# Moving the weight tiles by 128 bytes within each SBUF partition, in a fused state-space and mixture-of-experts layer

## What is computed

```python
x = _layernorm(x + attn(x))      # state-space part: z, Win, scan over 8 heads, gate, Wout
x = _layernorm(x + ffn(x))       # mixture of 12 experts, top 3 per token
# attn: z = x@Wz; X,B,C,dt = x@Win; y = ssd_scan(...) + D*X; (y * (silu(z)@Wzg)) @ Wout
# ffn, dense over the experts:
h = gelu(sum_e (x @ W1[e].T) * dw1[:, e])     # W1[e]: 512 x 128
y = sum_e (h @ W2[e].T) * dw2[:, e]           # W2[e]: 128 x 512
y = y + dw3 @ b2
```

## The kernel before, in words

| tile | start, bytes | modulo 256 | modulo 512 |
|---|---|---|---|
| before_lines | 16512 | 128 | 128 |
| w1_hi, w1_lo | 16640, 41216 | 0 | 256 |
| w2_hi, w2_lo | 65792, 90368 | 0 | 256 |
| wbc_hi, wbc_lo | 114944, 115456 | 0 | 256 |
| wz_hi, wz_lo | 115968, 116992 | 0 | 256 |
| wx_hi, wx_lo | 118016, 120064 | 0 | 256 |
| wzg_hi, wzg_lo | 122112, 126208 | 0 | 256 |
| wout (first tile after the weights) | 130304 | 0 | 256 |
| xT_hi, xT_lo | 141568, 143616 | 0 | 256 |
| fbuf (x1 is its first 2048 bytes) | 199168 | 0 | 0 |
| sp_hi, sp_lo | 209920, 218112 | 0 | 0 |
| dwpad | 227200 | 128 | 384 |
| a_hi, a_lo | 228192, 228320 | 96, 224 | 352, 480 |

## Time and profile before

### The profile page before, as it was taken

How to read it: one execution, slowest core, us unless ns; L and a number is a source line. 1 busy time by engine, 2 the same in 40 slices (tenths; PEclk the granted TensorE clock), 3 DMA queues, 4 the chain that set the end, 5 groups by cost and what they waited for, 6 DMA issues and landing times.

```text
span 1540.9 us, 25335 instructions
## 1 busy us (share of the span) xinstructions
PE 1525.7 (99%) x8646; PEld 1250.4 (81%) x8646; DVE 1115.0 (72%) x3113; ACT 598.1 (39%) x1360; POOL 658.3 (43%) x751
## 2 busy tenths in 40 slices
PE   9999999999999999999999999999999999999998
PEld 7778888888888888888788888888888888887886
DVE  7677776877768687686776768777686776767755
ACT  6643424425244351533525244242443515335130
POOL 6671623616145270643616336162451705436040
PEclk9999999999999999999999999999999999999999
DMA  6340312314023140321403123040230403214020
GB/s 180 100 148 29 118 42 67 100 29 135 18 77 90 30 137 15 103 71 46 120 11 125 45 61 106 28 132 21 72 95 29 138 15 96 76 39 128 14 78 7
DMA packets 81456, 114.53 MB, mean 74 GB/s; under 512 B 10144, under 2 KB 37296, under 8 KB 81328
## 3 DMA queue, kind: packets, MB, share of 16 engines
q1 hardware_dynamic: 81328, 112.92, 24.6%
HBM read 107.76 MB, written 5.13 MB: 73 GB/s over the span
## 4 chain that ended last, share of the span: by engine, by line
PE 93%; POOL 3%; DVE 1%; issue 1%; DMA 1%; SPq 0%; ACT 0%; POOLq 0%; DVEq 0%
PE exp_bank L247 23%; PE exp_bank L249 22%; PE exp_bank L248 22%; PE mix_bank L896 4%; PE mix_bank L922 3%; PE mix_bank L247 3%; PE mix_bank L249 3%; PE mix_bank L904 3%; PE mix_bank L248 3%; PE mix_bank L793 1%; PE turn_bank L1249 1%; PE mix_bank L525 1%; PE mix_bank L739 1%; PE mix_bank L1013 1%; POOL Wt L856 1%
## 5 line engine op out<-in xcount | busy, mean ns | idle before, releaser
L1190 POOL TENSOR_TENSOR sp_lo<-fbuf,sp_hi 128x512 fp32r<-128x512 f32 (+2 forms) x201 | 243.4, 1214 | 176.9 <-ACT sp_hi L1186 106.9
L247 PE MATMUL exp_bank<-w_hi,sp_hi 128*128 128x512 f32 x768 | 304.0, 396 | 0.8 <-POOL sp_lo L1242 0.8
L247 PE MATMUL exp_bank<-sp_hi,w_hi 128*128 128x512 f32 x764 | 303.5, 397 | 0.1
L249 PE MATMUL exp_bank<-w_hi,sp_lo 128*128 128x512 f32 x768 | 299.7, 390 | 0.0
L248 PE MATMUL exp_bank<-w_lo,sp_hi 128*128 128x512 f32 x768 | 298.9, 389 | 0.0
L249 PE MATMUL exp_bank<-sp_hi,w_lo 128*128 128x512 f32 x764 | 298.3, 391 | 0.0
L248 PE MATMUL exp_bank<-sp_lo,w_hi 128*128 128x512 f32 x764 | 297.8, 390 | 0.0
L1289 DVE SCALAR_TENSOR_TENSOR acc<-exp_bank,dw,acc 128x128 f32<-128x128 f32 x384 | 132.4, 345 | 137.2 <-PE exp_bank L249 136.6
L1186 ACT CAST sp_hi<-fbuf 128x512 fp32r<-128x512 f32 (+2 forms) x203 | 120.0, 592 | 272.5 <-DVE fbuf L1156 216.5
L856 POOL TENSOR_TENSOR Wt<-Wt,Gh 128x512 f32<-128x512 f32 x128 | 184.8, 1445 | 21.0 <-DVE Wt L848 21.0
L247 PEld LDWEIGHTS exp_bank<-sp_hi,w_hi 128*128 128x128 f32 x764 | 143.7, 188 | 38.2 <-issue 8.9
(11 more groups left out here) (267 smaller groups left out, 2286.1 us busy)
## 6 DMA issues: line engine op xcount, KB each, us to landing
row_b<-dw_rows SPq DMA_DIRECT2D x189, 256.0 KB, 3.3
seg_b<-dA_rows SPq DMA_DIRECT2D x124, 256.0 KB, 3.5
ctd<-cum_rows SPq DMA_DIRECT2D x128, 96.0 KB, 3.2
x_in<-in_x SPq DMA_DIRECT2D x16, 256.0 KB, 2.8
result<-acc SPq DMA_DIRECT2D x15, 256.0 KB, 2.2
fbuf<-in_W1T SPq DMA_DIRECT2D x12, 256.0 KB, 3.5
acc<-in_W2T SPq DMA_DIRECT2D x5, 256.0 KB, 3.5
x_in<-in_W2T SPq DMA_DIRECT2D x5, 256.0 KB, 2.8
```

Of the source, the lines that this page charges most:

```text
L247: nc.tensor.matmul(ps, s_hi, m_hi, start=start and j == 0, stop=False, skip_group_check=onto)
L249: last = nc.tensor.matmul(ps, s_lo, m_hi, start=False, stop=stop and j == n - 1, skip_group_check=onto)
L1190: sig("xw_lo", on.tensor_tensor(lo[:, cols], wide[e % 2][:, cols], hi[:, cols].bitcast(F32), ALU.subtract))
```

## The change

The number and the order of the tiles are kept, except for one unused tile of 128 bytes per partition. It stood ahead of the weights and now stands behind them.

```diff
@@ -91,7 +91,6 @@
-        sb("before_lines", [P, 32])
         w1_hi, w1_lo = sb("w1_hi", [P, E, HID], F32R), sb("w1_lo", [P, E, HID], F32R)
         w2_hi, w2_lo = sb("w2_hi", [P, NH, E * D], F32R), sb("w2_lo", [P, NH, E * D], F32R)
@@ -100,6 +99,7 @@
         wx_hi, wx_lo = sb("wx_hi", [P, DI], F32R), sb("wx_lo", [P, DI], F32R)
         wzg_hi, wzg_lo = sb("wzg_hi", [P, NK, DI], F32R), sb("wzg_lo", [P, NK, DI], F32R)
 
+        sb("half_line", [P, 32])
         wout = sb("wout", [P, NQ, D])
```

## The result

The changed kernel takes 1567.5 us (median of 4, 1567.48 to 1568.39), against 1542.8 us for the kernel before on the same chip: 24.7 us more, a ratio of 1.016 (95% interval 1.0148 to 1.0172). I had predicted no change, with a range that ended at 1547.8.

A forecast was written before the change was run, and what follows sets the result against it. PE was taken as the bound, with 5,328 fp32r matmuls at 226.7 ns making 1,208 us, 78% of the span. All terms were 0, so the forecast stayed at the median, 1543.3 us, range 1540.6 to 1547.8.

The forecast's parts named there:

- Terms 3 and 4: Splitting W1 and W2 once: 0, or 1.3 us without cover; tiles behind the weights, which keep their bytes: 0.
- term 2: Weights as moving operand, 2,496 matmuls: no change in start distance, 0; bounds -33 us to +4.2 us.
- term 1: Weights as stationary operand, 2,832 loads: no delay from the new position, 0; a third block's 156 us was excluded.
- load covered by 39 ns: Stationary loads take 188 ns, one starts every 226.7 ns, so 39 ns are free before a load delays a matmul.
- Rival B: Moving W2 or wx starting mid-block touches nine blocks, not eight: 1.7 ns each, 4.2 us, 1547.5 us; chance 0.12.
- dearer form: Rival B with the stationary side paying too: 1.7 ns on 5,328 matmuls, 9.1 us, 1552.4 us; within Rival B's 0.12.
- Rival A: TensorE's reads of both operands collide at present; half a block apart frees up to 71 us, 1472 us; chance 0.07.
- the 13.4 ns: Part of the 226.7 ns between fp32r matmul starts above the 213.3 ns that 512 columns take at 2.4 GHz.

The follow-up runs named there:

- the first map: Separate kernel computing none of the layer: streams of 44 fp32r matmuls, only the slices' start bytes varied; 226.6 ns at 256 and 0, 232.7 with the stationary at 128.

## Why the prediction was wrong

**What held.** The bound, the count and the sensitivity did: PE is the bound with and without the change, 5,328 fp32r matmuls carry it, and the loss is 4.9 ns on the distance between their starts. Terms 3 and 4 were 0: the growth of the distances accounts for the whole loss, and nothing behind the weights moved.

**The step that failed is term 2, and with it term 1.** Both were put at 0; the pairs of the trace give 12.0 us where the weight moves (term 2) and 13.8 us where it is stationary (term 1). In term 2 I took 0 because "the rows show the distance blind to position where they can tell". They couldn't tell. The rows compared differences of 0 and 256 bytes, and the first map has 226.6 ns at 256 (L44), as at 0, against 232.7 at 128 (L41). All fp32r rows of 512 columns of before had the same difference modulo 256, so they were one sample and not two. From that I should have drawn that no row tested the change.

**The nearest rows were of another kind.** Term 1 leaned on L1123, whose 512-byte stationary operand starts at 128 under a moving one at 0. It is a single float32 transpose beside other short matmuls, so it neither streams nor is fp32r. In the result its matmuls are at 272 ns, and float32 streams had 429 ns at both positions. Nor was its 1 ns a measure: its loads have a median of 143 ns in the result in place of 138, with both of its operands where they were. The load of the large matmuls stays at 188 ns in the changed kernel too. What changes is when the next matmul starts. I read "load covered by 39 ns" as "position of the stationary operand free"; only-W1-at-128 costs 12 us and shows that it isn't. The 39 ns were no measure of the cover either, since loads of 188 to 192 ns start 112 to 120 ns apart in streams of 128 and 256 columns.

**Rival B had the right sign and the wrong mechanism.** It let only moving operands pay, 1.7 ns for a ninth block. Taking the pad out puts all streams mid-block at no cost. The price was 4.9 ns and both roles paid it: 5,328 x 4.9 = 26 us, not 4.2. Even its dearer form, 1552.4 us, was 15 us short. Its remark that leaving equal positions "can lose a privilege which no row tests" was the true state of the evidence, and should have carried more chance and a wider upper end.

**Rival A and the page.** Half a block between the operands doesn't take the 13.4 ns away, and with 512 columns none of the 63 other positions gets below 226.7. Two reads that get in each other's way are not excluded by this: which offset is costly did turn out to depend on how the two operands lie to each other. The Trainium skill's "TensorE: Matmul & The Clock Gate" (Step-by-step: what each phase is for) says that loading the next tile's weights doesn't steal read bandwidth from the running matmul. No run measures the bandwidth, but the two operands are not independent in effect: moving only the start of W1, the stationary one, costs 6.6 ns a matmul in the stretch shown and 5.1 over its 2,304 matmuls. Whether that is the ports or something behind them, no run tells. The page's gap of N/2.4 + 2.5 ns (Back-to-back issue gap), 215.8 ns for 512 columns, wasn't reached at any position.

What stays open is the mechanism inside. Most settled distances are multiples of 6.67 ns (226.7, 233.3 and 240.0 are 34, 35 and 36 of them; 113.3, 120.0 and 173.3 are 17, 18 and 26), or are repeating patterns whose sum is one, as 229 + 238 = 467 = 70 x 6.67. That looks like a handover between matmuls that waits for its turn, but only the arithmetic points to it.

## What to carry to other kernels

Where fp32r matmuls of 512 columns run back to back and TensorE is the bound, start the stationary and the moving tile at equal bytes modulo 256: common starts at 0, 64, 128 and 192 all settled at 226.7 ns, and one small tile allocated between them was enough to lose 1 to 2% here. Before calling rows evidence that a quantity doesn't matter, check that they really differ in it, in the period that may count. The distance between starts shows the loss at once; PE's share of the span (99%) and of the chain (93%) doesn't. And the length of a load isn't the time that has to be free for it.

## What the runs showed of the hardware that I had not expected

- The cost depends on the difference of the two starts modulo 256, with its sign: 228.9 ns with the moving operand 64 above, 233.3 with it 192 above. The load's own time (188 ns) and the granted clock (1.00) don't show it.
- It isn't a matter of how far: 32 bytes off costs the layer 29 us, 128 bytes off 25 us.
- A stream has a memory. Behind streams at other positions the matmuls at equal starts needed up to ten to settle at 226.7 ns, once more than eleven, and at 240 bytes a stream settled at 226.7, 233.3 or 236.7 ns depending on what ran before.
- Loads overlap one another: each lasts 192 ns, and they start 111.7 ns apart in a stream of 128 columns.
- Halving the stationary columns made the distance longer (229.7 ns). With 256 moving columns, equal starts (120.0 ns) lose to 112 or 192 bytes (113.3 ns).
